# Late shared chunks: seven quarter products of 1024-token blocks in place of eight, with weights prepared on GpSimd

## What is computed

```python
router = xf @ gate_w.T
probs = softmax(router, axis=1)
top_p, top_i = top_k(probs, 2)
h = silu(einsum('nc,efc->enf', xf, expert_fc1)) * einsum('nc,efc->enf', xf, expert_fc2)
y = einsum('ne,enc->nc', combine, einsum('enf,ecf->enc', h, expert_proj))
s1 = xf @ shared_fc1.T
s2 = xf @ shared_fc2.T
shared = silu(s1) * s2 @ shared_proj.T
y = y + sigmoid(xf @ shared_gate_w.T) * shared
return x + y
```

## Time and profile before

| | us |
|---|---|
| median of three runs | 1295.43 |
| lowest, highest | 1293.08, 1296.06 |
| profiled execution, its span | 1294.0 |
| TensorE busy in it | 1277.8 (99%) |
| VectorE | 757.2 (59%) |
| ScalarE | 442.1 (34%) |
| GpSimd | 230.9 (18%) |

### The profile page before, as it was taken

The page is one execution under the profiler, slowest core; times in us unless marked ns, Lnnn a source line. Parts: engine busy times, 40 slices in busy tenths (PEclk is TensorE's granted clock), DMA queues, the critical chain, the costliest instruction groups (busy, mean ns, idle before and its releaser), DMA issues.

```text
span 1294.0 us, 20330 instructions
## 1 busy us (share of the span) xinstructions
PE 1277.8 (99%) x7150; PEld 1104.3 (85%) x7150; DVE 757.2 (59%) x1285; ACT 442.1 (34%) x744; POOL 230.9 (18%) x336
## 2 busy tenths in 40 slices
PE   6999999999999999999999999999999999999998
PEld 5888888888888989999999999998888888888886
DVE  5444443459645777777687677767535435445444
ACT  4323231121012666566566565555101101101100
POOL 4121220000001222212211221110122122122031
PEclk9999999999999999999999999999999999999999
DMA  9454544201235767777768766756152351351342
GB/s 317 125 196 144 203 126 163 106 33 66 98 124 186 273 248 257 267 260 261 264 238 279 269 224 242 254 212 220 60 163 60 103 162 48 114 162 43 120 130 65
DMA packets 84491, 222.72 MB, mean 172 GB/s; under 512 B 8578, under 2 KB 8706, under 8 KB 79458
## 3 DMA queue, kind: packets, MB, share of 16 engines
q1 hardware_dynamic: 73650, 186.77, 40.4%
q0 software_dynamic: 10800, 35.40, 10.0%
HBM read 169.97 MB, written 52.17 MB: 172 GB/s over the span
## 4 chain that ended last, share of the span: by engine, by line
PE 95%; DMA 2%; DVE 1%; issue 1%; SPq 1%; ACT 0%; POOLq 0%; POOL 0%; DVEq 0%
PE bank_h L644 60%; PE bank_o L644 29%; PE bank_t L634 2%; PE bank_t L644 2%; PE bank_t L591 1%; DMA rawp<-ewp 1%; PE bank_o L601 1%; PE bank_h L601 1%; DMA rawp<-swp 0%; DMA picked<-slot_rows,idx_stage 0%; PE bank_t L752 0%; DVE res L1333 0%; PE bank_h L853 0%; SPq L316 0%; DVE w_lo L1362 0%
## 5 line engine op out<-in xcount | busy, mean ns | idle before, releaser
L644 PE MATMUL bank_h<-x_hi,w_hi 128*128 128x256 f32 (+1 forms) x1480 | 499.6, 338 | 3.6 <-DVE x_lo L1370 2.8
L644 PE MATMUL bank_h<-x_hi,w_lo 128*128 128x256 f32 (+1 forms) x1480 | 493.3, 333 | 0.0
L644 PE MATMUL bank_h<-x_lo,w_hi 128*128 128x256 f32 (+1 forms) x1480 | 492.8, 333 | 0.0
L644 PEld LDWEIGHTS bank_h<-x_hi,w_hi 128*128 128x128 f32 x1480 | 273.4, 185 | 31.1 <-issue 4.7
L644 PEld LDWEIGHTS bank_h<-x_hi,w_lo 128*128 128x128 f32 x1480 | 273.3, 185 | 27.4
L644 PEld LDWEIGHTS bank_h<-x_lo,w_hi 128*128 128x128 f32 x1480 | 273.5, 185 | 26.4
L959 ACT ACTIVATE g_sb<-bank_h 128x512 f32<-128x512 f32 x88 | 52.6, 598 | 580.0 <-PE bank_h L644 580.0
L644 PE MATMUL bank_o<-wp_hi,h_hi 128*128 128x512 f32 (+1 forms) x565 | 229.4, 406 | 0.0
L1289 DVE TENSOR_TENSOR h_sb<-bank_h,g_sb 96x256 f32<-96x256 f32 (+1 forms) x184 | 101.3, 550 | 218.4 <-ACT g_sb L959 193.8
L644 PE MATMUL bank_o<-wp_lo,h_hi 128*128 128x512 f32 (+1 forms) x565 | 228.7, 405 | 0.0
L644 PE MATMUL bank_o<-wp_hi,h_lo 128*128 128x512 f32 (+1 forms) x565 | 227.5, 403 | 0.0
(11 more groups left out here) (154 smaller groups left out, 1134.3 us busy)
## 6 DMA issues: line engine op xcount, KB each, us to landing
raw<-ew SPq DMA_DIRECT2D x39, 1408.0 KB, 7.4
rawp<-ewp SPq DMA_DIRECT2D x39, 512.0 KB, 7.9
slot_rows<-res SPq DMA_DIRECT2D x32, 512.0 KB, 4.6
xt_in<-xf_transposed SPq DMA_DIRECT2D x15, 1024.0 KB, 8.3
picked<-x SPq DMA_DIRECT2D x32, 256.0 KB, 3.2
xf_rows<-rows SPq DMA_DIRECT2D x32, 256.0 KB, 3.3
res<-x SPq DMA_DIRECT2D x8, 1024.0 KB, 5.3
partial_rows<-res SPq DMA_DIRECT2D x8, 1024.0 KB, 4.2
```

The costliest lines, as they stand in the source:

```text
L644: mm = pe.matmul(dst, a, m, start=(first and i == 0), stop=(last and i == 2))
```

## The change

In the last pass the up-projection of a late chunk is done for 1024 tokens at a time (4 blocks in place of 8). The 512 channels are cut in two halves, the two halves of the width are fc1 and fc2, and the 1024 tokens are two halves of 512. Plain, that is 8 quarter products of 256 channels. The new scheme (Strassen's, in Winograd's form) makes 7 of sums: each is 2 channel slices x 3 = 6 matmuls of 512 columns. VectorE joins the seven results (u2, u3, c22, c21, c12), and one bank gets two products added up on TensorE. The names `P1, P6, P7, P5, P2, P4, P3` are in the order of execution.

- GpSimd makes the sums of the weights and their splits for all six chunks, in a new piece of its program between the last map copies and the first expert gather, and stores them to DRAM (`late_up`, `late_down`). Between chunks it waits for its own stores.
- In the last pass SyncE loads each product's split weights (256 KB) into a slot of its own, one chunk ahead: it waits until the product that used the slot is done. The down weights are loaded once for each of two teams of three chunks.
- GpSimd makes four sums of x per block of 1024 tokens, the first during the last expert steps, the next ones between the fourth and the fifth gather of the block. ScalarE and VectorE split the seven forms of x.
- The down-projection runs after every three chunks (a team), 8 rows of 3 products each, so the residual is added to twice per tile. Picks are added in the third chunk, in every second row of the first team and in the last three chunks.
- SyncE loads x of the first late block (2 MB) and three weight slots right after the second expert step.
- Loops of the last pass are written out.

```diff
+            def late_weights(j):
+                at, sums = j * (PRODUCTS + 1), 4 * j
+                a11, a12, a21, a22 = (raw_up[:, 2 * k:2 * k + 2, h, :] for h in range(2) for k in range(2))
+                s1, s2, s3, s4 = w_sum
+                pool.wait_ge(late.raw_in, 16 * (2 * j + 1))
+                at_least(pool, late.down_stored, 32 * j)
+                nc.gpsimd.tensor_tensor(s1, a21, a22, ALU.add).then_inc(late.summed, 1)
+                nc.gpsimd.tensor_tensor(s3, a11, a21, ALU.subtract).then_inc(late.summed, 1)
...
+                for q, source in enumerate((a11, s2, s3, s1)):
+                    late_slot(q, source, at + q)
+                pool.wait_ge(late.split_lo, at + 4)
+                nc.gpsimd.dma_start(late_up[j, :, 0:4 * SLOT], rows_flat[:, :]).then_inc(late.up_stored, 16)
+                pool.wait_ge(late.up_stored, 32 * j + 16)
+                wp_raw = rows_flat[:, 3 * SLOT:4 * SLOT]
+                nc.gpsimd.dma_start(wp_raw, swp[PARTS[1][j]]).then_inc(late.raw_in, 16)
+                for q, source in enumerate((a12, a22, s4)):
+                    late_slot(q, source, at + 4 + q)
...
+            late_raw(0)
+            for j in range(LATE):
+                late_weights(j)
+            pool.wait_ge(late.up_stored, 32 * LATE)
+            pool.wait_ge(late.down_stored, 32 * LATE)
             pool.wait_ge(routing_done, 1)
...
+                for r in range(HROWS):
+                    if r == BT and b + 1 < HBLOCKS:
+                        late_sums(b + 1)
+                    gather_slots(HROWS * b + r)
...
+            def late_chunk(n):
+                bank_a, bank_b, bank_d, bank_c, bank_e = *bank_t, *bank_h[0:3]
...
+                at_least(pe, late.g1, n)
+                late_product(n, P1, bank_a, True)
+                at_least(pe, late.u2, n)
+                late_product(n, P6, bank_b, True)
+                at_least(pe, late.u3, n)
+                late_product(n, P7, bank_d, True)
+                at_least(pe, late.c12, n)
+                late_product(n, P5, bank_c, True)
+                pe.wait_ge(late.p1_kept, n + 1)
+                late_product(n, P2, bank_a, False)
+                at_least(pe, late.c21, n)
+                late_product(n, P4, bank_e, True)
+                pe.wait_ge(late.c22, n + 1)
+                late_product(n, P3, bank_c, False)
...
+            def late_chunk(n, pick=None):          # VectorE's part
+                nc.vector.tensor_tensor(u2_sb, bank_t[1][:, :], p1_sb, ALU.add).then_inc(late.u2, 1)
...
+                nc.vector.tensor_tensor(u3_sb, bank_h[0][:, :], u2_sb, ALU.add).then_inc(late.u3, 1)
...
+                nc.vector.tensor_tensor(h2_sb, bank_h[1][:, :], u3_sb, ALU.add).then_inc(late.c22, 1)
+                if pick is not None:
+                    late_pick(pick)
...
+                nc.vector.tensor_tensor(h1_sb, u3_sb, bank_h[2][:, :], ALU.subtract).then_inc(late.c21, 1)
...
+                nc.vector.tensor_tensor(h1_sb, h1_sb, g1_sb, ALU.mult).then_inc(late.h1, 1)
...
+                nc.vector.tensor_tensor(g2_sb, bank_h[1][:, :], u2_sb, ALU.add).then_inc(late.c12, 1)
...
+                nc.vector.tensor_tensor(late_h[1][:, jj, 0:BN], h1_sb, late_h[0][:, jj, 0:BN], ALU.subtract).then_inc(late.h_lo, 1)
...
+                nc.vector.tensor_tensor(h2_sb, h2_sb, g2_sb, ALU.mult).then_inc(late.h2, 1)
...
+                nc.vector.tensor_tensor(late_h[1][:, jj, BN:HB], h2_sb, late_h[0][:, jj, BN:HB], ALU.subtract).then_inc(late.h_lo, 1)
...
+            def late_row(b, g, r):
+                at_least(pe, late.o_kept, (b * TEAMS + g) * HROWS + r - 1)
+                for jj in range(TEAM):
+                    j = g * TEAM + jj
+                    if r % BT == 0:
+                        pe.wait_ge(late.h_lo, 2 * (b * LATE + j) + r // BT + 1)
...
+                    if n + 1 < HBLOCKS * LATE:
+                        for p in range(PRODUCTS):
+                            sp.wait_ge(late.p_full, PRODUCTS * n + p + 1)
+                            load_late_w((j + 1) % LATE, p)
+                    if b and j == 0:
+                        load_late_res(b)
```

More of the change, by code:

```diff
@@ L83 @@
 CHOICES = 2 * TILES
+PRODUCTS = 7
+P1, P6, P7, P5, P2, P4, P3 = range(PRODUCTS)
+LATE = len(PARTS[1])
+TEAM = 3
+TEAMS = LATE // TEAM
+HB = 2 * BN
+HROWS = HB // P
+HBLOCKS = TOKENS // HB
+SLOT = 2 * 2 * P
 GRP = 8
@@ L460, in _ @@
                 whole_step(u, u, u)
+            sp.wait_ge(shared[0].x_lo, BLOCKS - 1)
+            load_late_x(0)
+            sp.wait_ge(late.up_stored, 2 * 16 * LATE)
+            for p in (P1, P6, P7):
+                load_late_w(0, p)
             with sp.Fori(0, GROUPS) as g:
@@ L481, in _ @@
[L481 to L489 removed]
+            store_whole(XT - 2, XT - 2 - SINGLE, 1)
+            sp.wait_ge(late.down_stored, 2 * 16 * LATE)
@@ L911, in _ @@
+            for b in range(HBLOCKS):
+                for g in range(TEAMS):
+                    for jj in range(TEAM):
+                        late_chunk(b * LATE + g * TEAM + jj)
+                    if b == 0:
+                        pe.wait_ge(late.wp_in[g], 32)
+                        if g == 0:
+                            pe.wait_ge(ex.o_kept, 2 * XT)
+                    for r in range(HROWS):
+                        late_row(b, g, r)
         @block.scalar
@@ L1099, in _ @@
             act.wait_ge(ex.o_full, 2 * (XT - 1))
[L1100 to L1102 removed]
+            late_x_hi(0, P1)
+            late_x_hi(0, P6)
+            for j, p in enumerate((P7, P5, P2)):
                 expert_gate(XT - 1, j)
[L1104 to L1107 removed]
+                late_x_hi(0, p)
@@ new lines, in late_pick @@
+            def late_pick(t):
+                r = t % HROWS
+                if r % BT == 0:
+                    dve.wait_ge(late.res_in[r // BT], 16 * (t // HROWS + 1))
+                dve.wait_ge(picked_in[t % 2], 32 * (t // 2 + 1))
+                for k, done in enumerate((pick_half, picked_used)):
+                    nc.vector.scalar_tensor_tensor(out=late_res(r), in0=picks[:, t % 2, k, :], scalar=p_top[:, k, t:t + 1],
+                                                   in1=late_res(r), op0=ALU.mult, op1=ALU.add).then_inc(done, 1)
+                    dve.wait_ge(done, t + 1)
```

407 lines of the change are left out of this document (292 added, 115 removed).

## The result

The changed kernel takes 1329.1 us (median; 1324.7 to 1331.4) where the kernel before took 1295.7 beside it on the same chip: ratio 1.0261, interval 1.0246 to 1.0277, so 33 us slower. The forecast was 1317 and slower. The profiled execution has a span of 1328.4.

The account below looks back on a forecast made before the run. TensorE, busy 99% of the span, was taken as the bound, so each new wait counts in full: 1294.0 - 33.8 + 23 + 2 + 4 + 26 = 1315, with 1.4 for the median 1317 us; range 1278 to 1360.

Parts of the forecast that it names:

- Removed, 33.8: Late up-projection and end of span: 144 fewer matmuls save 32.6 us, a shorter end 1.2; 33.8 in all.
- Preparation, 23 + 2 at the turn: Before the experts: GpSimd needs 30.5 us per chunk, so TensorE waits 23 us for gathered rows, plus 2 of clock.
- my own list: Signs of a wrong forecast: GpSimd done before 400, late stage shorter than 365 us, or weights waited for in every chunk.
- The wait for the lock, 5 us per chunk: Weight preparation: 26 GpSimd instructions per chunk each wait 0.2 us for VectorE, adding 5 us to 25.4.
- The upper bound: Preparation at listed instruction prices: 44 us per chunk, GpSimd's end at 504, TensorE wait of 104 us.
- Experts, 4: Expert stage: the 2.75 MB load ahead of the fifth expert's weights costs 4 us, bounds 0 and 8, first sums included.
- Late stage, 26: Late chunks: group edges 6, first group's row stage 15, weights behind bursts 5; sum 26 us, bounds 8 and 60.
- The clock: Granted clock falls after TensorE waits: 2 us added after the 23 us wait, none for the late stage.
- Rival (4): Late stage: the clock falls at each of nine waits, 1.4 us each, 12 in all, giving 1329; chance 0.06.
- Rival (1): GpSimd's preparation done in time and late-stage edges cheap (12 to 18 us), giving 1281; chance 0.22.
- (2): Preparation: GpSimd much slower, 38 us per chunk, end 468, wait 68, giving 1362; chance 0.15.
- (3): Late stage bound by streamed weights or gathers, 2.5 us in each of 24 chunks, 60 us, giving 1351; chance 0.12.

Follow-up runs that it names:

- stores_only: Changed kernel without GpSimd's sums and splits of the late weights, its loads and stores kept: 1316.8 us, ratio 1.0176.
- v2_late_prep: v1_spread with GpSimd's weight preparation moved from before the experts into the six expert groups: 1328.5 us, ratio 1.0249.
- v1_spread: Changed kernel with the 2.75 MB burst and first sums spread over expert steps, first partial-sum load later, later sums behind the gathers: 1304.9 us, ratio 1.0082.

## Why the prediction came out as it did

The direction and the range were right; the sum is 12 us short and its terms are not the measured ones.

- **Removed, 33.8.** Right. The 144 matmuls are gone. Inside a group a chunk takes 9.52 us (first products at 1034.14 and 1043.66), and the last matmul starts 3.7 us before the end.
- **Preparation, 23 + 2 at the turn.** Measured 9.9, of which 1.3 were already there at the last logits product. GpSimd took 26.8 per chunk, not 30.5, and issued its last store at 397.62, before 400: by my own list that step was wrong, if narrowly, for in kernels with the same preparation a chunk took 26.7 to 28.4 and the last store came between 394 and 407. The operation of 256 elements took 0.73 (0.62 taken), a copy 0.40 (0.33), a store issue 0.55 (1.1 taken, from the gathers). The wait for the lock, 5 us per chunk, was too much: over the six chunks GpSimd's arithmetic was busy for 90.4 us where these undisturbed times make 76, so 2.3 per chunk. Two things went the other way: 13.4 us from the issue of the last store to the first gather where I had 1.1, and VectorE's lengthened routing steps, which I had counted at nothing because the wait at the turn would swallow them. It did not: they cost 7.1 and the gather itself 1.6 (stores_only took back 12.3). The upper bound was also added up wrongly: its terms make 35 us per chunk (40 with the waits for VectorE) and not 44, so a wait of 51 (82) and not 104; no sum or chance used it.
- **Experts, 4.** Measured 16.6: a wait of 7.3 for the burst, one of 5.1 for the first sums, and the clock behind each, 5 together. I had put the sums "inside this figure". Bounds 0 to 8 did not hold.
- **Late stage, 26.** The waits are 26.7: 2.6 over eight group edges (6 taken), 9.1 for weights (5 taken), 15 for sums and gathers (15 taken), at the places named: row 7 of the first group in three blocks (7.9), the third bank at the fourth chunk (in one block, 5.0), the second chunk's weights (6.5). But the stage lost 41.7; 5 more are gaps too short for that list.
- **The clock.** Rival (4), held at 0.06 because the waits would be short, is the rest: the granted clock fell to 0.50 at the waits of 5 us and more and also at two of 3.2, and cost about 9 in the late stage (that rival had 12), besides 5 in the experts and 2 in the preparation, where 2 had been put. The forecast lies within 12 us of the result by luck: the preparation was 15 too dear, the experts 13 and the late stage 16 too cheap. That forecast plus that rival make 1329 is luck for the same reason. The Trainium skill (TensorE: Matmul & The Clock Gate, "HAM oscillation — how this bites in real kernels") describes these falls after idle gaps; the rows above agree, and I should have given that rule more than six in a hundred, having forecast a wait of 23 us and four or five of 3 to 5.
- **Rival (1)** asked for less than 27 us per chunk on GpSimd and less than 30 lost in the late stage. The first was so (26.8), the second not (41.7). **(2) and (3)** fell: 26.8 against 38 per chunk; no wait for weights in 20 of 24 chunks.

What the cause was, then: 42 us from GpSimd's arithmetic (12.3 + 29.8) and 9.0 from streamed weights, shown by taking them away one after another. Another 13 were still there at the end of that series, in the experts where the burst stands and at the edges of the groups; that the burst in pieces costs nothing to be seen is shown by v1_spread. Some 3 us of the 67 (33.4 and the 33.8 removed) belong to no single edit. That GpSimd works by holding VectorE up is read from the fences and from VectorE's busy time. The Trainium skill (SBUF — State Buffer, "SBUF: two separate sides") calls the port pair of the two engines an exclusive lock held for the whole instruction. It names VectorE's operations with two SBUF inputs and its fast modes as those that need the pair. The fence at 891 to 904 us agrees: the splits and the cast stood until a GpSimd instruction ended, the product that reads a PSUM bank did not. With the sums on VectorE there is no such instruction left to stand for, and those runs gained.

## What to carry to other kernels

Price an idle engine's work by what it does to the busy one beside it: sixteen sums of 2.4 to 2.75 us on average on GpSimd cost 30 us; made by VectorE, though that was the engine at 70 to 75%, and put where it had room, they left the late stage as short (380.4) as in the kernels with the sums cut (381.1 and 383.6). Price a wait with the clock behind it: in the late stage here 26.7 us of waits brought 8.6 of clock, and waits of 3.2 us had their part in it. A burst can cost more than its own transfer where each step loads just in time (up to 9.5 us for 2.75 MB here): cut it to pieces and give one to each step before moving it elsewhere.

## What the runs showed of the hardware that was not expected

- 3.86 us pass between GpSimd's first index copy and the first gather behind it, with nothing the profile shows as awaited. stores_only has them too (copy 380.21, gather 384.25). The kernel before has 0.91 there and v2_late_prep 0.94, both without a preparation ahead of this gather. What it is was not tried.
- 4.6 to 9.5 us pass between the last store of the preparation and the index copy. The program waits there for its own last stores, which land after about 3 us; what the rest is was not tried either.
- A GpSimd subtraction took 0.73 us for 256 columns, 1.28 for 512 and 2.40 for 1024; VectorE's took 1.22 for 1024. A plain DMA issued by GpSimd takes 0.55 of it, a gather about 1.0.
- The streamed weights cost the late stage 11.3 us (381.1 against 369.8) while the mean traffic was 222 GB/s; with the other loads cut to 1 MB no wait for weights is left at 225 GB/s (late stage 375.6). So those waits came from the order of the loads and not from their bytes alone.
